# Joined attention and routing stage: the two copies of the values and the routed rows take turns on ScalarE, and the maxima of the experts move ahead of an addition on VectorE

## The chip, the cores and the metric

One core of a Trainium2 chip runs the whole kernel. The metric is the device time of one execution in microseconds (us). The engines are TensorE (PE in the profile, with PEld for its weight loads), VectorE (DVE), ScalarE (ACT), GpSimd (POOL) and the queues that issue DMAs. Each engine runs its own list of instructions in order, and semaphores hold an instruction until another engine has signalled.

## The reference

Four images of 3136 tokens with 192 features pass through a tokenizer with softmax attention, and then through blocks that add to a residual `h`. The stage of this change computes the second block and the choice of experts of the third:

```python
# linear attention with a decay, added to h
q = (elu(x @ Wq) + 1) * scale; k = elu(x @ Wk) + 1; v = x @ Wv
c = clip(cumsum(log(sigmoid(x @ Wf + bf))), -20, 20)
numerator   = q . (exp(c) * cumsum(exp(-c) * k v^T))
denominator = q . (exp(c) * cumsum(exp(-c) * k)) + 1e-6
h = h + layernorm(numerator / denominator) @ Wo
# router of the mixture of experts, on the normalised h
routing = softmax(gelu(x @ w1 + b1) @ w2 + b2)      # 8 experts
topv, topi = top_k(routing, 2)
```

The experts themselves, a second attention and a last feed-forward block follow in later stages.

## The kernel before

The joined stage is `attend_route_phase`. It cuts the 12544 tokens into 28 chunks (`NC`) of 448 tokens (`CH`), each of four tiles (`TPC`) of 112 tokens. Every engine has a loop `for g in range(NC + 3)` that is written out in full, and the order of its calls is the order of the engine. In turn g the engines work on several chunks at once: attention on chunk g, the projections of chunk g+1, the normalised rows for the router (`normalise_route`, tile `xr`) of chunk g-1, the router's matmuls of chunk g-2, and the choice of experts (`choose`, `take_rank`, `places`) of chunk g-3.

What the change and the steps of the prediction touch:

- **ScalarE.** `take_n` copies the transposed attention output (`nT`). `decay` makes `dec`, which VectorE's `q_and_k` needs. `values_out(g, i)` copies half i of the values from the accumulator `pvo` to `vt`; its signal `v_out` also frees `pvo` for TensorE's next `wo_out`. `take_ex` makes the exponentials of the router's softmax. `normalise_route` writes four tiles of `xr` and copies a part of them (L957), and signals `xr_ready`. `states` copies the running state out of `pst` into `snap`, four times in a turn, and `high_x` (L1004) takes the transposed input of the next chunk.
- **TensorE.** `values` (L790) is two halves of ten matmuls. Then `wo_out` for the first two tiles (L843), `weights` (L799), `transpose_r` (L856, waits for `xr_ready`), `wo_out` for the last two tiles (L843 again), `attend` for two tiles (L820, L822, L825), `transpose_x` (L765), `rank` (L884 to L889), `attend` for the other two, `router` and `project`. Within `attend` each tile waits for the state's copy of the tile before, and its last matmul signals `num_mm`.
- **VectorE.** `mask_weights` (L1151), `add_out(g-1, 0)` (L1159), which waits for GpSimd's `rst`, `choose` (L1206 to L1216), `add_out(g-1, 1)` (L1159), which waits for the second `wo_out`, `add_bias` (L1167, adds `brow` to `h`), the statistics, `take_rank` (L1228, waits for `rank`), `low_x`, and `sums_out` (L1095, waits for `num_mm`).
- **GpSimd.** The routed rows of chunk g-4 go to memory by eight indirect DMAs (L723) in a turn, two batches of four. One batch runs after `idx` is written; `factor` (the two instructions that make `rst`) follows it, and then the second batch.

Of the kernel before, what the change touches and what calls it, by code (L numbers as in the profile page):

```python
# [17 lines left out]
D = 192  # L18
# [5 lines left out]
TPC = CH // T  # L24
# [529 lines left out]
def attend_route_phase(nc, ins, h, bns, mean, rstd, minus, eye, held, gate, slot, shift, tile_e, tile_r, down,  # L554
# [5 lines left out]
    G3 = 3  # L560
    with ExitStack() as ctx:
# [93 lines left out]
        R = {n: sem(f"{n}_3") for n in route_names}  # L655
# [4 lines left out]
        def here(g):  # L660
            return 0 <= g < NC
# [266 lines left out]
        def _(act):  # L928
# [13 lines left out]
                    act.wait_ge(S["xn_half"], g + 1)  # L942
                    nc.scalar.copy(xn[g % 2][:, :, D:256], xn[g % 2][:, :, 128:D]).then_inc(S["xn_ready"], 1)

            def normalise_route(r):

                act.wait_ge(R["off_out"], r + 1)
                if r >= G3:
                    act.wait_ge(scattered[r % G3], 16 * 2 * TPC * (r // G3))
                x = xr[r % G3]  # L950
                for q in range(TPC):
                    t = r * TPC + q
                    ac = nc.scalar.activation(x[:, q, 0:D], h[:, t, :], ACT.Identity, bias=minus[:, t:t + 1],
                                              scale=rstd[:, t:t + 1])
                ac.then_inc(R["half_out"], 1)
                act.wait_ge(R["half_out"], r + 1)
                nc.scalar.copy(x[:, :, D:256], x[:, :, 128:D]).then_inc(R["xr_ready"], 1)  # L957

            def take_r(r):
                act.wait_ge(R["rtr_mm"], r + 1)  # L960
# [25 lines left out]
            def values_out(g, i):  # L986
                act.wait_ge(S["v_mm"], 2 * g + i + 1)
                nc.scalar.copy(vt[:, 2 * i:2 * i + 2, 0:D],
                               pvo[:, i, 0:2 * VS].rearrange("p (q v) -> p q v", q=2)[:, :, 0:D]).then_inc(
                                   S["v_out"], 1)  # L990

            def decay(g):
                act.wait_ge(S["cum_out"], g + 1)
                nc.scalar.activation(dec[:], cum[:], ACT.Exp, scale=sgn[:]).then_inc(S["dec_out"], 1)
# [30 lines left out]
            for g in range(NC + 3):  # L1025
                if here(g):
                    keys_out(g)
                if here(g + 2):
                    normalise(g + 2, (0,))
                if here(g - 2):  # L1030
                    take_r(g - 2)
                if here(g + 2):
                    normalise(g + 2, (1,))
                if here(g):
                    states(g, (0,))
                if here(g + 2):
                    normalise(g + 2, (2,))
                if here(g):
                    states(g, (1,))
                if here(g + 2):  # L1040
                    normalise(g + 2, (3,))
                if here(g + 1):
                    high_x(g + 1)
                if here(g):
                    states(g, (2, 3))
                if here(g - 2):
                    take_hidden(g - 2)
                if here(g + 1):
                    gate(g + 1)
                if here(g):  # L1050
                    take_n(g)
                if here(g + 1):
                    decay(g + 1)
                    for i in range(2):
                        values_out(g + 1, i)
                if here(g - 2):
                    take_ex(g - 2)
                if here(g - 1):
                    normalise_route(g - 1)
                if g < 2:  # L1060
                    high(g)

        @block.vector
        def _(dve):
# [84 lines left out]
            def mask_weights(g):  # L1149
                dve.wait_ge(S["at_mm"], g + 1)  # L1150
                nc.vector.tensor_tensor(at[:, :, :], pat[:, 0:CH].rearrange("p (q t) -> p q t", q=TPC),  # L1151
                                        mask[:, :].unsqueeze(1).broadcast_to([T, TPC, T]), ALU.mult).then_inc(S["at_out"], 1)
# [47 lines left out]
                nc.vector.tensor_tensor(lg[:], logit, peak[:].broadcast_to([T, TPC, E]),  # L1200
                                        ALU.subtract).then_inc(R["lg_out"], 1)

            def choose(r):

                dve.wait_ge(R["ex_out"], r + 1)
                nc.vector.tensor_reduce(total[:, :, 0], ex[:], AX.X, ALU.add)  # L1206
                for q in range(TPC):
                    mx = nc.vector.max(top[:, q, :], ex[:, q, :])
                link(mx)
                nc.vector.tensor_tensor(both[:], top[:, :, 0:1], top[:, :, 1:2], ALU.add)  # L1210
                for q in range(TPC):
                    mx = nc.vector.max_index(which[:, q, :], top[:, q, :], ex[:, q, :])
                link(mx)
                link(nc.vector.tensor_tensor(pick[:], number[:].unsqueeze(1).unsqueeze(1).broadcast_to([T, TPC, 2, E]),
                                             which[:, :, 0:2].unsqueeze(3).broadcast_to([T, TPC, 2, E]), ALU.is_equal))
                nc.vector.tensor_tensor(sel[:], pick[:, :, 0, :], pick[:, :, 1, :], ALU.add).then_inc(R["sel_out"], 1)  # L1216
# [69 lines left out]
            for g in range(NC + 3):  # L1286
                if here(g):
                    mask_weights(g)
                if here(g - 1):
                    add_out(g - 1, 0)  # L1290
                if here(g - 3):
                    choose(g - 3)
# [1330 lines left out]
```

## Time and profile before

| | |
|---|---|
| median of three runs | 2784.31 us (2782.99 to 2789.03) |
| profiled execution | 2790.76 us, of which span 2788.9 us |
| busy share: PE, DVE, ACT, POOL | 82%, 72%, 56%, 36% |
| `weights` to the last `idx` of the joined stage | about 880 to 1456 us of the span |
| TensorE's granted clock between 965.92 and 1319.41 us | 1.00 of full speed |
| VectorE, TensorE busy there, of 353.49 us | 307.11 us, 317.11 us |

The profile is of one execution. A row of its timeline gives the start of an instruction or a run of equal ones, its duration, and in brackets how long its engine sat idle before it and who ended the wait. "issue" and "remote" as the one who ended it mean that the profile found no releasing instruction close enough in time. The matmuls' ends are modelled.

### The profile page before, as it was taken

To read this page: it belongs to the slowest core of one execution; us is meant where nothing else is said; L and a number is where in the kernel's file an instruction comes from. 1 tells how busy PE (TensorE), PEld (TensorE's weight loads), DVE (VectorE), ACT (ScalarE), POOL (GpSimd) and SP (SyncE) were. 2 spreads that over 40 slices of the span, in tenths; PEclk is the share of its full clock that TensorE was granted. 3 is DMA by queue.
4 is the path that set the end of the run, shared out by engine and by line. 5 is a ranking of instruction groups with operands and counts; after the bars stand their busy time and mean duration, and the time that the engine had idled before them with its cause. 6 is when DMAs were issued, how large, how long until landed. Compare 5 with 4: busy or idle time off the path is not lost. (4 is left out here: it accounts for less than half of the span.)

```text
span 2788.9 us, 45419 instructions
## 1 busy us (share of the span) xinstructions
PE 2293.3 (82%) x14046; PEld 1665.0 (60%) x14047; DVE 2000.3 (72%) x5437; ACT 1550.6 (56%) x2693; POOL 996.8 (36%) x1024
## 2 busy tenths in 40 slices
PE   8999999999996888989865999926678885666665
PEld 4444444444444878888854999925576774444443
DVE  5777777777764888888853444447788877889986
ACT  2444444444444777777743566536665650777776
POOL 1100100100000355555561444468776730444443
PEclk9999999999997999999976999966787887677867
DMA  2000000000002011111125777731111100000000
GB/s 56 0 18 12 0 18 13 0 9 1 0 1 89 21 47 47 47 50 46 51 79 190 256 256 256 256 101 50 47 48 42 49 13 22 21 21 26 26 25 26
DMA packets 69143, 162.81 MB, mean 58 GB/s; under 512 B 12977, under 2 KB 32342, under 8 KB 68702
## 3 DMA queue, kind: packets, MB, share of 16 engines
q1 hardware_dynamic: 39426, 94.27, 10.3%
q0 software_dynamic: 21504, 44.99, 5.6%
q10 hardware_dynamic: 8064, 21.68, 2.6%
q8 instruction: 79, 1.29, 0.2%
q14 instruction: 70, 0.57, 0.1%
HBM read 63.98 MB, written 63.88 MB: 46 GB/s over the span
## 5 line engine op out<-in xcount | busy, mean ns | idle before, releaser
L211 ACT ACTIVATE prob<-pscore 128x896 f32<-128x896 f32 x336 | 308.1, 917 | 424.1 <-PE pscore L293 424.1
L418 DVE TENSOR_REDUCE pmax<-ppre 112x1 f32<-112x512 f32 x656 | 424.4, 686 | 162.7 <-PE ppre L260 162.6
L307 PE MATMUL pout<-prob,xkey 128*64 128x448 f32 x1344 | 328.3, 567 | 0.4 <-ACT prob L211 0.4
L260 PE MATMUL ppre<-xh,yh 49*112 49x512 f32 x656 | 291.5, 446 | 7.8 <-DVE pmax L418 4.1
L723 POOL DMA_INDIRECT rows_in<-xr,idx x224 | 231.4, 1033 | 154.4 <-DVE idx L1237 97.3
L1694 POOL DMA_INDIRECT yg<-rows_out,place x224 | 234.2, 1045 | 62.4 <-issue 62.1
L193 POOL CAST yh<-ynext 113x448 fp32r<-113x448 f32 x28 | 17.2, 616 | 668.1 <-DVE pmax L418 639.9
L260 PEld LDWEIGHTS ppre<-xh,yh 49*112 49x112 f32 x656 | 112.8, 172 | 239.8 <-issue 103.5
L293 PE MATMUL pscore<-yh,xh 49*128 49x448 f32 x700 | 241.3, 422 | 0.4 <-DVE yh L438 0.4
L2209 POOL TENSOR_TENSOR yg<-y,gout 112x512 f32<-112x512 f32 x112 | 141.3, 1273 | 259.1 <-DVE y L2442 259.1
L1544 POOL TENSOR_TENSOR zl<-z,zh 128x448 fp32r<-128x448 f32 x126 | 144.8, 1149 | 219.8 <-ACT zh L1510 210.3
L293 PE MATMUL pscore<-yh,xl 49*128 49x448 f32 x700 | 202.7, 364 | 0.0
L1564 DVE COPY yb<-py 112x384 f32<-112x384 f32 x126 | 70.2, 558 | 103.5 <-PE py L1472 103.4
L1458 PE MATMUL pz<-xth3b,wd 128*128 128x448 f32 x504 | 143.5, 387 | 0.0
L293 PE MATMUL pscore<-yl,xh 49*128 49x448 f32 x700 | 143.3, 364 | 0.0
L1772 PE MATMUL pqk<-xh,wh 128*128 128x448 f32 x168 | 76.9, 458 | 74.5 <-ACT junk L1915 34.8
L2254 PE MATMUL pyt<-eyeb,yq 112*128 112x112 bf16 x448 | 43.7, 285 | 111.5 <-ACT yq L2330 111.5
L1472 PE MATMUL py<-uph,zh 128*112 x504 | 130.9, 260 | 1.2 <-POOL zl L1544 1.2
L1472 PE MATMUL py<-upl,zh 128*112 x504 | 131.6, 261 | 0.0
L1472 PE MATMUL py<-uph,zl 128*112 x504 | 131.5, 261 | 0.0
L307 PEld LDWEIGHTS pout<-prob,xkey 128*64 128x64 f32 x1344 | 66.6, 135 | 106.0 <-issue 85.6
L293 PEld LDWEIGHTS pscore<-yh,xl 49*128 49x128 f32 x700 | 128.2, 187 | 0.8
(388 smaller groups left out, 6558.2 us busy)
## 6 DMA issues: line engine op xcount, KB each, us to landing
wd<-down SPq DMA_DIRECT2D x63, 512.0 KB, 3.0
xb<-rows_in SPq DMA_DIRECT2D x63, 448.0 KB, 3.6
rows_out<-yb ACTq DMA_DIRECT2D x63, 336.0 KB, 3.2
out<-ho SPq DMA_DIRECT2D x28, 336.0 KB, 2.8
rows_in<-zero SPq DMA_DIRECT2D x15, 448.0 KB
rows_in<-xr,idx POOLq DMA_INDIRECT x224
yg<-rows_out,place POOLq DMA_INDIRECT x224
xkey<-in_xkey SPq DMA_DIRECT2D x4, 800.0 KB, 6.7
```

Source lines behind the costliest of these rows:

```text
L211: nc.scalar.activation(prob[j % 3][:, :, :], pscore[j % 2][:, :, 0:CH], ACT.Exp).then_inc(exped, 1)
L260: pe.matmul(out[:, :], yh1[rows, q * T:(q + 1) * T], xh[b % 2][rows, block * 512:(block + 1) * 512], start=True, stop=True, tile_position= ...
L293: mm = pe.matmul(pscore[j % 2][:, i, 0:CH], x[b % 2][rows, keys], y[rows], start=(n == 0), stop=(n == 2), tile_position=(i * LO, 0))
L307: mm = pe.matmul(pout[i * LO:(i + 1) * LO, 0:CH], xkey[b % 2][:, 2 * j + i, :], prob[j % 3][:, i, :], start=(j == 0), stop=(i == 1 and j = ...
L418: nc.vector.reduce_max(pmax[:, q, 2 * block + half:2 * block + half + 1], bank(u, depth), AX.X).then_inc(pre_max, 1)
L723: nc.gpsimd.indirect_dma_start(rows_in, bass.IndirectOffsetOnAxis(ap=idx[r % G3][:, 2 * q + k:2 * q + k + 1], axis=0), xr[r % G3][:, q, :] ...
L1458: mm = pe.matmul(pz[m][:, 0:CH], wd[i][:, w, cols], x, start=(s_ == 0), stop=(s_ == 4))
L1472: mm = pe.matmul(py[i][:, q // 2, (q % 2) * D:(q % 2 + 1) * D], zz[i][m][:, cols], w[:, bass.ds(2 * e + m, 1), :], start=(m + n == 0), sto ...
L1544: nc.gpsimd.tensor_tensor(zl[i][m][:], z[m][:], zh[i][m][:].bitcast(F32), ALU.subtract).then_inc(S["zl_out"], 1)
L1694: nc.gpsimd.indirect_dma_start(yg[g % 2][:, q, k, :], None, rows_out, bass.IndirectOffsetOnAxis(ap=place[:, c:c + 1], axis=0)).then_inc(ga ...
L1772: mm = pe.matmul(pqk[m % 2][:, 0:CH], w, x, start=(n == 0), stop=(n == 4))
L2209: nc.gpsimd.tensor_tensor(yg[:, q, :], y[:, q, :], gout[:], ALU.mult).then_inc(S["yg_out"], 1)
```

## The change

On ScalarE the first copy of the values goes ahead of the decay. `normalise_route` is cut in two, tiles 0 and 1 and tiles 2 and 3, and the second copy of the values goes between them. The exponentials of the router (`take_ex`) so come ahead of the second copy. On VectorE the head of `choose` becomes a function of its own, `largest`: the sum of the exponentials, the eight largest of each tile and the sum of the two largest. It goes ahead of `add_out(g-1, 0)`. No instruction is added or taken away.

```diff
-            def normalise_route(r):
+            def normalise_route(r, tiles):
 
-                act.wait_ge(R["off_out"], r + 1)
-                if r >= G3:
-                    act.wait_ge(scattered[r % G3], 16 * 2 * TPC * (r // G3))
+                if 0 in tiles:
+                    act.wait_ge(R["off_out"], r + 1)
+                    if r >= G3:
+                        act.wait_ge(scattered[r % G3], 16 * 2 * TPC * (r // G3))
                 x = xr[r % G3]
-                for q in range(TPC):
+                for q in tiles:
...
-                ac.then_inc(R["half_out"], 1)
-                act.wait_ge(R["half_out"], r + 1)
-                nc.scalar.copy(x[:, :, D:256], x[:, :, 128:D]).then_inc(R["xr_ready"], 1)
+                if TPC - 1 in tiles:
+                    ac.then_inc(R["half_out"], 1)
+                    act.wait_ge(R["half_out"], r + 1)
+                    nc.scalar.copy(x[:, :, D:256], x[:, :, 128:D]).then_inc(R["xr_ready"], 1)
...
                 if here(g + 1):
+                    values_out(g + 1, 0)
                     decay(g + 1)
-                    for i in range(2):
-                        values_out(g + 1, i)
                 if here(g - 2):
                     take_ex(g - 2)
                 if here(g - 1):
-                    normalise_route(g - 1)
+                    normalise_route(g - 1, (0, 1))
+                if here(g + 1):
+                    values_out(g + 1, 1)
+                if here(g - 1):
+                    normalise_route(g - 1, (2, 3))
...
-            def choose(r):
+            def largest(r):
...
                 nc.vector.tensor_tensor(both[:], top[:, :, 0:1], top[:, :, 1:2], ALU.add)
+
+            def choose(r):
+
                 for q in range(TPC):
                     mx = nc.vector.max_index(which[:, q, :], top[:, q, :], ex[:, q, :])
...
                 if here(g):
                     mask_weights(g)
+                if here(g - 3):
+                    largest(g - 3)
                 if here(g - 1):
                     add_out(g - 1, 0)
```

On ScalarE, at the end of one turn in the middle of the stage, this stood before (`vt` are the values, `xr` the routed rows, `ktok` the keys of the next turn):

```order
L975 COPY nT<-ptr 96x896
L994 ACTIVATE dec<-cum,sgn 128x448
L988 COPY vt<-pvo 112x2x192 x2
L971 ACTIVATE ex<-lg 112x32
L953 ACTIVATE xr_1<-h,minus,rstd 112x192 x4
L957 COPY xr_1<-xr_1 112x4x64
L998 COPY ktok<-pff 112x4x64
```

and this stands there now:

```order
L977 COPY nT<-ptr 96x896
L990 COPY vt<-pvo 112x2x192
L996 ACTIVATE dec<-cum,sgn 128x448
L973 ACTIVATE ex<-lg 112x32
L954 ACTIVATE xr_1<-h,minus,rstd 112x192 x2
L990 COPY vt<-pvo 112x2x192
L954 ACTIVATE xr_1<-h,minus,rstd 112x192 x2
L959 COPY xr_1<-xr_1 112x4x64
L1000 COPY ktok<-pff 112x4x64
```

One copy of the values moved up past the decay, the other down past `ex` and two tiles of `xr`.

On VectorE, at the start of a turn, this stood before (`at` are the masked weights, `top` and `which` the largest values and their places):

```order
L1151 TENSOR_TENSOR at<-pat,mask 112x448
L1159 SCALAR_TENSOR_TENSOR h<-pvo,rst,h 112x192 x2
L1206 TENSOR_REDUCE total<-ex 112x4
L1208 MAX top<-ex 112x8 x4
L1210 TENSOR_TENSOR both<-top 112x4
L1212 MAX_INDEX which<-top,ex 112x8 x4
L1214 TENSOR_TENSOR pick<-number,which 112x64
L1216 TENSOR_TENSOR sel<-pick 112x32
L1159 SCALAR_TENSOR_TENSOR h<-pvo,rst,h 112x192 x2
L1167 TENSOR_TENSOR h<-h,brow 112x768
```

and this stands there now:

```order
L1156 TENSOR_TENSOR at<-pat,mask 112x448
L1211 TENSOR_REDUCE total<-ex 112x4
L1213 MAX top<-ex 112x8 x4
L1215 TENSOR_TENSOR both<-top 112x4
L1164 SCALAR_TENSOR_TENSOR h<-pvo,rst,h 112x192 x2
L1220 MAX_INDEX which<-top,ex 112x8 x4
L1222 TENSOR_TENSOR pick<-number,which 112x64
L1224 TENSOR_TENSOR sel<-pick 112x32
L1164 SCALAR_TENSOR_TENSOR h<-pvo,rst,h 112x192 x2
L1172 TENSOR_TENSOR h<-h,brow 112x768
```

Three groups of short instructions moved up past the first addition to `h`; the second addition and all behind it keep their order. The lists of TensorE and GpSimd are as they were.

## Rows read from the trace of the kernel before

**Rows 1.** Timeline of VectorE, one turn: start us, duration us, instruction, [idle before, releaser].

```profile
1306.88 0.62 DVE L1146 SCALAR_TENSOR_TENSOR qt<-elu,dec 64x448 f32<-64x448 f32 x1
...
1310.70 0.74 DVE L1159 SCALAR_TENSOR_TENSOR h<-pvo,rst,h 112x192 f32<-112x192 f32 x2 [0.37 <-POOL rst L705]
1311.36 0.17 DVE L1206 TENSOR_REDUCE total<-ex 112x4 f32<-112x32 f32 x1
...
1311.93 0.09 DVE L1212 MATCH_VALUE_LOAD which<-top,ex 112x8 f32 x1
...
1313.54 0.74 DVE L1159 SCALAR_TENSOR_TENSOR h<-pvo,rst,h 112x192 f32<-112x192 f32 x2 [0.48 <-issue]
1314.32 0.96 DVE L1167 TENSOR_TENSOR h<-h,brow 112x768 f32<-112x768 f32 x1
...
1317.32 0.19 DVE L1228 TENSOR_TENSOR pos<-pat,run 112x32 f32<-112x32 f32 x1 [0.45 <-PE pat L889]
...
1319.41 0.23 DVE L1095 TENSOR_SCALAR den<-pvo 112x2 f32<-112x2 f32 x2 [0.39 <-PE pvo L825]
```

**Rows 2.** Timeline of ScalarE around the same turn's start.

```profile
1306.11 0.67 ACT L994 ACTIVATE dec<-cum,sgn 128x448 f32<-128x448 f32 x1 [0.58 <-issue]
1306.69 0.46 ACT L988 COPY vt<-pvo 112x384 f32<-112x384 f32 x1
1308.31 0.48 ACT L988 COPY vt<-pvo 112x384 f32<-112x384 f32 x1 [1.16 <-remote]
1308.69 0.23 ACT L971 ACTIVATE ex<-lg 112x32 f32<-112x32 f32 x1
1308.82 1.85 ACT L953 ACTIVATE xr<-h,minus,rstd 112x192 f32<-112x192 f32 x4
1310.70 0.41 ACT L957 COPY xr<-xr 112x256 f32<-112x256 f32 x1
```

**Rows 3.** Timeline of TensorE, same stretch; the first two rows end the halves of `values`.

```profile
1305.42 0.27 PE L790 MATMUL pvo<-wxl,xh 128*112 128x192 f32 x1
...
1306.40 0.26 PE L790 MATMUL pvo<-wxl,xh 128*112 128x192 f32 x1
1307.29 1.53 PE L843 MATMUL pvo<-wo,nT 96*112 96x192 f32 x8 [0.63 <-ACT vt L988]
...
1311.16 0.97 PE L856 MATMUL ptr<-eye,xr 112*96 112x112 f32 x8 [1.12 <-ACT xr L957]
...
1313.27 0.49 PE L820 MATMUL pst<-vt,ktok 112*128 112x193 f32 x2
```

**Rows 4.** Timeline of GpSimd: last indirect DMA of one batch, first and last of the next.

```profile
1306.52 0.94 POOL L723 DMA_INDIRECT rows_in<-xr,idx  x1 [0.31 <-issue]
...
1310.87 1.00 POOL L723 DMA_INDIRECT rows_in<-xr,idx  x1 [0.20 <-issue]
...
1314.67 1.43 POOL L723 DMA_INDIRECT rows_in<-xr,idx  x1 [0.30 <-issue]
```

**Rows 5.** Timeline of ScalarE, a turn before any indirect DMA.

```profile
935.42 0.84 ACT L988 COPY vt<-pvo 112x384 f32<-112x384 f32 x2
```

**Rows 6.** Timeline of all engines in turn 4, the first with indirect DMAs.

```profile
957.63 1.00 POOL L723 DMA_INDIRECT rows_in<-xr,idx  x1 [0.20 <-issue]
...
958.75 0.49 PE L820 MATMUL pst<-vt,ktok 112*128 112x193 f32 x2
...
960.51 0.96 DVE L1167 TENSOR_TENSOR h<-h,brow 112x768 f32<-112x768 f32 x1
...
960.75 0.93 PE L765 MATMUL ptr<-eye,xn 112*128 112x112 f32 x8
961.43 0.95 POOL L723 DMA_INDIRECT rows_in<-xr,idx  x1 [0.30 <-issue]
...
963.46 0.91 ACT L1004 CAST xh<-ptr 128x896 fp32r<-128x896 f32 x1 [1.97 <-remote]
...
965.92 0.23 DVE L1095 TENSOR_SCALAR den<-pvo 112x2 f32<-112x2 f32 x2 [0.26 <-PE pvo L825]
```

## The prediction

> **What bounds the kernel now.** I read the stage from its timeline, one engine after the other, over one turn of the loop, because the change only moves instructions inside a turn. A turn is the distance between two starts of `sums_out`. It starts at 965.92 us in turn 4 [rows 6] and at 1319.41 us in turn 22 [rows 1], so 18 turns take 353.49 us and one takes 19.64 us. The reader should see that no engine fills the turn alone. VectorE is nearest to it. It waits 0.37 us for GpSimd's `rst`, 0.48 us ahead of the second addition, 0.45 us for the rank and 0.39 us for the last attention matmul [rows 1]. What ends last there is a chain through ScalarE and TensorE. The second copy of the values starts at 1308.31, `ex` and the four tiles of `xr` follow, then the copy L957 at 1310.70, and TensorE, idle for 1.12 us, starts `transpose_r` at 1311.16 [rows 2, 3]. 2.11 us after it comes `attend` at 1313.27, and 6.14 us later `sums_out` [rows 3, 1].
>
> The head of this chain is odd. The last matmul of the second half of `values` ends at 1306.66, but the copy that waits for it starts at 1308.31, after 1.16 us of idle ScalarE [rows 3, 2]. In a turn without indirect DMAs the two copies run back to back [rows 5]. So TensorE's signal reaches ScalarE 1.65 us late while GpSimd is at its fourth indirect DMA, which starts at 1306.52 [rows 4], and the copy starts 1.79 us after that. I call this a held signal. It shows again in turn 4. `transpose_x` ends at 961.68 and the cast that waits for it starts at 963.46, after 1.97 us of idle, 2.03 us behind the start of that batch's fourth DMA at 961.43 [rows 6].
>
> **The change, part by part.**
>
> Second copy behind two tiles of `xr`. ScalarE has nothing to do while the signal is held. Now `ex` and two tiles go there: 0.13 us for `ex` (1308.69 to 1308.82), and (1310.70 - 1308.82) / 4 = 0.47 us for a tile [rows 2]. That is 1.07 us, and it fits between the decay's end and 1308.31. Behind the copy stand only two tiles: 1308.31 + 0.38 + 0.94 = 1309.63 for L957, and 0.46 us later, 1310.09, `transpose_r` can start. That is 1.07 us earlier than 1311.16. TensorE is then just through with the keys (1311.16 - 1.12 = 1310.04), so the whole amount counts. `attend` moves from 1313.27 to 1312.20. Every DMA issue keeps its place, since ScalarE issues none here. If the signal of the second half were not held, the copy would not be late, and the floor would be TensorE at about 1310.0, which is the same.
>
> First copy ahead of the decay. The decay starts at 1306.11 and `q_and_k` at 1306.88, only 0.10 us behind its end [rows 1, 2]. The first half of the values is computed at 1305.69 [rows 3]. If its signal comes at once, the copy is out of the way at 1306.07 and the decay loses nothing. If it is held too, the decay waits for up to the 0.58 us between two such starts. I take 0.2 us, nearer to the lower bound, because the first half ends before the fourth DMA starts. This falls on the path: `q_and_k`, the mask, `rst` and the second batch of DMAs (1310.87 to 1311.07) all move by it. What it gives is the 0.63 us that TensorE waits for the copy [rows 3]. That lies beside VectorE's own work until the mask, so I give it nothing.
>
> Maxima ahead of the addition. They cost 1311.93 - 1311.36 = 0.57 us and fill the 0.37 us wait for `rst`. Without that wait the first addition would start at 1310.70 - 0.37 = 1310.33. With the maxima ahead of it and the 0.2 us it starts at 1311.10, 0.4 us later than before; `attend` needs it at 1312.20, and its 0.74 us end at 1311.84, so it is hidden, by 0.36 us. Before, it took 0.66 us to the next instruction (1310.70 to 1311.36), and the rest of `choose` ran from 1311.93 to the wait at 1313.54 - 0.48 = 1313.06, that is 1.13 us [rows 1]. So the second addition starts at 1311.10 + 0.66 + 1.13 = 1312.89, 0.65 us ahead of 1313.54, and no longer waits: its matmuls move by 1.07 us. The rank is ready 1.07 us earlier as well.
>
> Sum before any new wait: `sums_out` at 1319.41 - 1.07 = 1318.34, so a turn of 19.64 - 1.07 = 18.6 us. VectorE alone would allow 19.64 - 0.37 - 0.48 - 0.45 - 0.39 + 0.2 = 18.15 us, so it does not stand in the way. There are 23 turns, 5 to 27, at about 1 us: 23 us.
>
> **What is late next.** `attend` now starts 1312.20 - 1311.07 = 1.13 us behind the first DMA of the second batch. Before it started 2.40 us behind it [rows 3, 4], so half of its signals fell behind the batch. In turn 4 the distance was 958.75 - 957.63 = 1.12 us, the same as it will be, because there the second copy was not yet held [rows 6]. And that turn was no shorter: `sums_out` came 8.29 us behind the first DMA (before: 8.54), 7.17 us behind `attend` instead of 6.14. The held signal of `transpose_x` took it all.
>
> One thing differs from turn 4. `add_bias` (L1167) reads two operands from on-chip memory, and with the maxima moved it starts at 1312.89 + 0.78 = 1313.67, just as the third DMA of the batch starts. The fourth started 3.80 us behind the first [rows 4], and a step is 1.25 us (0.94 us and 0.31 us of idle), so the third is due at 1311.07 + 2.55 = 1313.62. In the turn of the rows it ran until 1315.28, 0.61 us into the fourth DMA, and that one took 1.43 us and not 0.94; in turn 4 it ended as the fourth started, and that took 0.95 us [rows 1, 4, 6]. So 0.49 us for 0.61 us of overlap. With 0.96 us of overlap, the third DMA takes some 0.75 us more and the fourth starts at 1315.6. The Trainium skill, SBUF — State Buffer, "Who interferes with whom", says that a VectorE instruction with two inputs in SBUF contends with a GpSimd instruction that reads SBUF. The trace agrees with that for 1.43 against 0.94 us. By the page alone the price would end there, on GpSimd, and the turn would be 18.6 us; it gives no wait to TensorE's signals.
>
> **Forecast.** `transpose_x` signals in the stretched third DMA and passes or waits little. In turn 4 it started 2.00 us behind `attend` and took 0.93 us [rows 6]; the rank's matmuls and the third state's follow within about a microsecond, so that state ends about 1316.1, half a microsecond into the fourth DMA. I take it to be held to 1315.6 + 1.79 = 1317.4. Its copy comes where turn 4's came behind the cast: 965.92 - 963.46 = 2.46 us less the cast's 0.91 us leaves 1.55 us to `sums_out` [rows 6]. So `sums_out` comes at 1318.95, 0.46 us ahead of 1319.41. With turn 4's 2.03 us in place of 1.79 us it is 0.22 us. I take 0.3 us, and 23 turns make 7 us. In the stage's tail the maxima fall into a wait for `rst`, which I put at 0.5 us once, about their own length. The profiled execution took 2790.76 us, 6.45 us over the median of the runs, and the sum holds as a difference against either: 2784.3 - 7.5 = 2777 us. A measurement of this kernel tells about 0.2%, 5.6 us, from no change.
>
> **Rivals.**
>
> 1. Full gain: the stretched DMA shifts the holds and no signal that matters is caught. For it: in turn 4 `attend` ran from 958.75 to `transpose_x` at 960.75 without a hold, in the second and third DMA [rows 6]. Against: the fourth DMA caught the signal in both places above. A turn of 18.3 to 18.9 us, 17 to 30 us in all, with 23 us at its middle: 2761 us.
> 2. All taken back, as in turn 4: `sums_out` 8.29 us behind 1311.07, at 1319.36, within 0.1 us of now: 2784 us, give or take 2. For it speaks turn 4. Against it, its DMAs were not stretched.
> 3. Slower. If a signal is held until the fourth DMA has been under way for 2.03 us, and `transpose_x` is caught already in the stretched third, the cast starts at 1315.6 + 2.03 = 1317.65, and 2.46 us later, at 1320.1, comes `sums_out`. That is 0.7 us later than 1319.41, 16 us in 23 turns: 2800 us. It decides as soon as `transpose_x`'s signal, due at about 1315.1, waits for the fourth DMA. For it: in turn 4 the same signal was held, 0.25 us behind the fourth DMA's start. Against: none of the rows shows a long hold that begins ahead of it.
> 4. The reordering does nothing, because the second copy waits anyway and the first two tiles of `xr` wait for something else, `off_out` or the old rows' DMAs. Against: in the turn of the rows `xr` started the moment `ex` let it [rows 2], and nothing it needs is moved. 2784 us.
>
> **How the numbers follow.** Forecast 0.38 (2772 to 2783), full gain 0.24, all taken back 0.20, slower 0.14, nothing 0.04. Six tenths of the first and all of the second are faster by over 0.2%: 0.46. Slower: the 0.14 and 0.04 from a larger delay of the decay (0.4 us in 23 turns is 9 us) on top of the third: 0.18. Within 0.2%: 0.36. The range leaves out the better half of the full gain below, and most of the slower case above: 2758 to 2792 us.
>
> **What would show it.** In the profile after: `attend` starts 1.1 us behind the first DMA of the second batch, and not 2.4 us; ScalarE's idle of 1.16 us ahead of the second copy shrinks to 0.2 or 0.3 us; VectorE's waits for `rst` and ahead of the second addition are gone; the third DMA of the second batch takes 1.7 us; a wait of over 1 us, with "remote" or "issue" as releaser, stands ahead of the third `snap` copy or of the cast. The prediction is wrong if held signals do not follow the DMAs, or if the mean distance of two `sums_out` is outside 19.1 to 19.5 us.

## The result, and the profile after

The changed kernel takes 2764.45 us (median of four runs, 2763.42 to 2765.61); the kernel before, on the same chip, 2786.26 us (four runs, 2782.99 to 2789.03). The ratio is 0.9918, with a 95% interval of 0.9904 to 0.9932: 21.8 us faster. The profiled execution took 2763.42 us, of which the span is 2761.6 us.

| distance of two `sums_out` | before | after |
|---|---|---|
| turn 0 to 4 | 75.95 us | 78.22 us |
| turn 4 to 22, each | 19.64 us (965.92 to 1319.41) | 18.42 us (967.32 to 1298.90) |
| turn 22 to 27, each | 19.47 us | 18.04 us |

So 23 turns gave 29.1 us (450.85 us before, 421.78 us after), and the first four gave back 2.3 us. The last `sums_out` starts 27.7 us earlier, and the span is 27.3 us shorter. Of that, 4.50 us are the amount by which the profiled execution of before (2790.76 us) lay over the median of 2786.26 us, and 1.03 us the amount by which that of after lay under its own.

The timeline of VectorE in one turn after the change, which answers to [rows 1]:

```profile
1280.72 0.23 DVE L1100 TENSOR_SCALAR den<-pvo 112x2 f32<-112x2 f32 x2 [0.18 <-PE pvo L825]
...
1288.27 0.62 DVE L1151 SCALAR_TENSOR_TENSOR qt<-elu,dec 64x448 f32<-64x448 f32 x1 [0.26 <-ACT dec L996]
...
1292.20 0.74 DVE L1164 SCALAR_TENSOR_TENSOR h<-pvo,rst,h 112x192 f32<-112x192 f32 x2
...
1293.95 0.74 DVE L1164 SCALAR_TENSOR_TENSOR h<-pvo,rst,h 112x192 f32<-112x192 f32 x2
1294.72 0.96 DVE L1172 TENSOR_TENSOR h<-h,brow 112x768 f32<-112x768 f32 x1
...
1297.18 0.16 DVE L1236 TENSOR_TENSOR pos<-pat,run 112x32 f32<-112x32 f32 x1
...
1298.90 0.23 DVE L1100 TENSOR_SCALAR den<-pvo 112x2 f32<-112x2 f32 x2 [0.19 <-PE pvo L825]
```

ScalarE in the same turn, which answers to [rows 2]:

```profile
1287.12 0.48 ACT L990 COPY vt<-pvo 112x384 f32<-112x384 f32 x1 [0.51 <-PE pvo L790]
1287.50 0.67 ACT L996 ACTIVATE dec<-cum,sgn 128x448 f32<-128x448 f32 x1
1288.07 0.22 ACT L973 ACTIVATE ex<-lg 112x32 f32<-112x32 f32 x1
1288.19 0.97 ACT L954 ACTIVATE xr<-h,minus,rstd 112x192 f32<-112x192 f32 x2
1289.39 0.48 ACT L990 COPY vt<-pvo 112x384 f32<-112x384 f32 x1 [0.23 <-remote]
1289.77 0.99 ACT L954 ACTIVATE xr<-h,minus,rstd 112x192 f32<-112x192 f32 x2
1290.79 0.40 ACT L959 COPY xr<-xr 112x256 f32<-112x256 f32 x1
...
1293.88 0.32 ACT L1011 COPY snap<-pst 128x193 f32<-128x193 f32 x1 [0.28 <-PE pst L820]
```

TensorE, which answers to [rows 3]:

```profile
1291.24 0.97 PE L856 MATMUL ptr<-eye,xr 112*96 112x112 f32 x8 [0.20 <-ACT xr L959]
...
1293.36 0.49 PE L820 MATMUL pst<-vt,ktok 112*128 112x193 f32 x2
```

And GpSimd, the fourth indirect DMA of one batch, and the first, third and fourth of the next, which answers to [rows 4]:

```profile
1287.60 0.94 POOL L723 DMA_INDIRECT rows_in<-xr,idx  x1 [0.30 <-issue]
...
1292.25 0.99 POOL L723 DMA_INDIRECT rows_in<-xr,idx  x1 [0.20 <-issue]
...
1294.79 1.69 POOL L723 DMA_INDIRECT rows_in<-xr,idx  x1 [0.30 <-issue]
1296.79 0.94 POOL L723 DMA_INDIRECT rows_in<-xr,idx  x1 [0.30 <-issue]
```

Read it from the `sums_out` of the turn before, which starts at 1280.72 us here and at 1299.64 us in the kernel before. The decay comes 6.78 us behind it (before 6.47), `transpose_r` 10.52 us (11.52), `attend` 12.64 us (13.63), the next `sums_out` 18.18 us (19.77). So 0.99 us were won up to `attend`, and 0.60 us between `attend` and `sums_out` (5.54 us, before 6.14). The second copy still starts 1.79 us behind the fourth DMA, as in [rows 2, 4], but only 0.23 us of that is idle now.

The 0.60 us are in the first state's copy. It starts 0.52 us behind `attend` after the change. Before it started 1.12 us behind, with 0.87 us of idle ahead of it, and TensorE waited for it in turn:

```profile
1314.39 0.32 ACT L1009 COPY snap<-pst 128x193 f32<-128x193 f32 x1 [0.87 <-PE pst L820]
```

```profile
1314.76 0.59 PE L820 MATMUL pst<-vt,ktok 112*128 112x193 f32 x2 [0.34 <-issue]
```

```profile
1313.42 0.94 POOL L723 DMA_INDIRECT rows_in<-xr,idx  x1 [0.30 <-issue]
```

These three rows are of the kernel before: ScalarE, TensorE, and GpSimd's third DMA. By the normal 0.52 us the copy was due at 1313.79, inside that DMA. The first state's copy waited like this in eight of the 18 turns before; in the other ten it was the second state's copy, with 0.62 to 0.66 us of idle where 0.24 us is normal.

The third state is the one that the forecast let wait. In the turn of the rows above, TensorE, then ScalarE:

```profile
1296.63 0.57 PE L820 MATMUL pst<-vt,ktok 112*128 112x193 f32 x2
```

```profile
1297.24 0.32 ACT L1011 COPY snap<-pst 128x193 f32<-128x193 f32 x1
```

Its matmuls end (modelled) at 1297.20 us, 0.41 us into the fourth DMA, and the copy starts at once. It is so in 14 of the 18 turns: the copy starts 0.4 to 0.6 us behind the start of the fourth DMA.

In the four others the distance was 19.03 to 19.08 us. In three of them the forecast's hold is to be seen. ScalarE and GpSimd in the turn that ends at 1096.82 us:

```profile
1093.66 0.91 ACT L1006 CAST xh<-ptr 128x896 fp32r<-128x896 f32 x1 [0.53 <-PE ptr L765]
1095.18 0.32 ACT L1011 COPY snap<-pst 128x193 f32<-128x193 f32 x1 [0.62 <-PE pst L820]
```

```profile
1091.83 1.70 POOL L723 DMA_INDIRECT rows_in<-xr,idx  x1 [0.30 <-issue]
1093.83 0.94 POOL L723 DMA_INDIRECT rows_in<-xr,idx  x1 [0.31 <-issue]
```

The third state's copy starts 1.35 us behind the fourth DMA, and the turn is 0.8 us longer than its neighbours. I find nothing in its rows ahead of the cast that tells it from them.

The fourth long turn, which ends at 1189.51 us, is different. VectorE pauses for 0.26 us without a known reason ahead of the second addition to `h`, so that `add_bias` starts inside the third DMA and not just ahead of it. That DMA is then not stretched, the fourth starts 3.80 us behind the first instead of 4.54 us, and the signal of `transpose_x` is held. VectorE, GpSimd, ScalarE:

```profile
1184.80 0.96 DVE L1172 TENSOR_TENSOR h<-h,brow 112x768 f32<-112x768 f32 x1
```

```profile
1184.53 0.94 POOL L723 DMA_INDIRECT rows_in<-xr,idx  x1 [0.30 <-issue]
1185.78 0.94 POOL L723 DMA_INDIRECT rows_in<-xr,idx  x1 [0.30 <-issue]
```

```profile
1187.02 0.91 ACT L1006 CAST xh<-ptr 128x896 fp32r<-128x896 f32 x1 [1.20 <-PE ptr L765]
```

### The profile page after: what moved, and what is told of

It is laid out like the page before. It is cut to its first block and busy times, and to the rows that moved or that the text cites. A ratio compares the mean times of both kernels' runs of the same rounds, so it can differ in the third digit from the quotient of the medians.

```text
span 2761.6 us, 45420 instructions
## 1 busy us (share of the span) xinstructions
PE 2304.1 (83%) x14046; PEld 1669.4 (60%) x14047; DVE 1995.4 (72%) x5437; ACT 1551.1 (56%) x2693; POOL 1001.9 (36%) x1024
## 3 DMA queue, kind: packets, MB, share of 16 engines
q8 instruction: 79, 1.29, 0.2%
## 5 line engine op out<-in xcount | busy, mean ns | idle before, releaser
L723 POOL DMA_INDIRECT rows_in<-xr,idx x224 | 237.8, 1062 | 132.3 <-DVE idx L1245 73.8
```

Of the source, the lines that this page charges most:

```text
L723: nc.gpsimd.indirect_dma_start(rows_in, bass.IndirectOffsetOnAxis(ap=idx[r % G3][:, 2 * q + k:2 * q + k + 1], axis=0), xr[r % G3][:, q, :] ...
```

## The experiments

Twelve measurements of nine kernels in four sessions, each session on one chip, with runs of the kernel before beside them. "Turn" is the mean of 18 turns between the two starts of `sums_out` given (turn 4 and 22).

| session | kernel | median us | before us | ratio (95%) | starts | turn |
|---|---|---|---|---|---|---|
| A, chip 10 | ScalarE's part alone | 2747.41 | 2745.80 | 1.0004 (0.9989 to 1.0018) | 967.99, 1292.68 | 18.04 |
| A | maxima alone | 2745.79 | 2745.80 | 1.0006 (0.9991 to 1.0021) | 963.81, 1286.05 | 17.90 |
| A | second copy and maxima | 2748.65 | 2745.80 | 1.0011 (0.9999 to 1.0023) | 964.32, 1286.55 | 17.90 |
| A | first copy and maxima | 2743.16 | 2745.80 | 0.9990 (0.9972 to 1.0007) | 965.39, 1282.89 | 17.64 |
| B, chip 11 | before, no indirect DMAs | 2741.96 | 2779.55 | 0.9862 (0.9831 to 0.9893) | 964.38, 1289.08 | 18.04 |
| B | changed, no indirect DMAs | 2740.65 | 2779.55 | 0.9863 (0.9832 to 0.9894) | 965.85, 1286.70 | 17.83 |
| B | changed, one-input `add_bias` | 2772.88 | 2779.55 | 0.9972 (0.9955 to 0.9989) | 966.66, 1305.82 | 18.84 |
| B | changed, `split_low` late | 2750.43 | 2779.55 | 0.9893 (0.9865 to 0.9921) | 958.33, 1282.87 | 18.03 |
| C, chip 11 | changed | 2756.72 | 2784.43 | 0.9910 (0.9887 to 0.9934) | 965.46, 1290.73 | 18.07 |
| C | first copy and maxima | 2768.81 | 2784.43 | 0.9949 (0.9935 to 0.9963) | 963.21, 1296.59 | 18.52 |
| D, chip 10 | maxima alone | 2780.32 | 2782.57 | 0.9997 (0.9980 to 1.0013) | 964.24, 1313.57 | 19.41 |
| D | second copy and maxima | 2750.09 | 2782.57 | 0.9881 (0.9859 to 0.9904) | 963.80, 1288.49 | 18.04 |

**Session A: the parts.** Four kernels between the two. ScalarE's part alone puts the maxima back:

```diff
                 if here(g - 1):
                     add_out(g - 1, 0)
                 if here(g - 3):
+                    largest(g - 3)
                     choose(g - 3)
```

> The changed kernel with the maxima back behind the first addition, so ScalarE's part alone. Theory: the whole gain (21.8 us) comes from the second copy of the values leaving the head of the chain to transpose_r, and the maxima only fill a wait of VectorE that nothing needed. Then 17 to 22 us faster than before, a turn of 18.4 to 18.7 us. Rival: the gain needs the shifted add_bias, which stretches the third indirect DMA of the second batch. With the maxima back, add_bias starts some 0.4 us later, the overlap falls partly into the fourth DMA, and signals are held again: 5 to 12 us faster, a wait of over 1 us ahead of the cast or of a snap copy in most turns.

The maxima alone have ScalarE's order of before: `decay`, both copies, `take_ex`, the four tiles.

> The kernel before with the maxima moved, so VectorE's part alone. Theory: the second addition still waits for the second wo_out, behind transpose_r, so nothing on the path moves: within 4 us of before. Rival: the rank is ready earlier and the turn ends on VectorE, where 0.37 us of waiting for rst goes away: 5 to 9 us faster.

"Second copy and maxima" puts the first copy back:

```diff
                 if here(g + 1):
-                    values_out(g + 1, 0)
                     decay(g + 1)
+                    values_out(g + 1, 0)
```

> The changed kernel with the first copy of the values back behind the decay; the second stays between the tiles of xr. Theory: the second copy carries the gain, and the first copy's place costs the decay 0.26 us a turn and gives nothing: 20 to 28 us faster than before, as fast as the changed kernel or up to 6 us faster. Rival: the first copy ahead of the decay lets TensorE start wo_out 0.6 us earlier and that is part of the gain: 10 to 16 us faster.

"First copy and maxima" puts the second copy back:

```diff
                     values_out(g + 1, 0)
                     decay(g + 1)
+                    values_out(g + 1, 1)
...
-                    normalise_route(g - 1, (0, 1))
-                if here(g + 1):
-                    values_out(g + 1, 1)
-                if here(g - 1):
-                    normalise_route(g - 1, (2, 3))
+                    normalise_route(g - 1, (0, 1, 2, 3))
```

> The changed kernel with the second copy of the values back ahead of ex and the four tiles; the first copy stays ahead of the decay, the maxima stay moved. Theory: the second copy is held by TensorE's late signal as before, so the head of the chain is as before and the decay's delay is the only other effect: between 3 us faster and 6 us slower than before. Rival: the first copy's place is part of the gain: 5 to 12 us faster.

None of the four can be told from the kernel before, and that kernel takes 2745.8 us here (median of 35), 40 us less than where the result was measured. The first and third expectation failed; the second and fourth held, but here they would have held for any cause. With ScalarE's order of before, the two copies run back to back beside the fourth DMA. ScalarE, then GpSimd, in a turn of the maxima alone:

```profile
1167.15 0.67 ACT L996 ACTIVATE dec<-cum,sgn 128x448 f32<-128x448 f32 x1 [0.58 <-DVE cum L1137]
1167.73 0.84 ACT L990 COPY vt<-pvo 112x384 f32<-112x384 f32 x2
```

```profile
1167.56 0.94 POOL L723 DMA_INDIRECT rows_in<-xr,idx  x1 [0.30 <-issue]
```

The fourth DMA takes its 0.94 us as ever, but no signal is late. Of the kernel before there is no trace from session A, only its time. I read this as two conditions, with held signals or without; without them the change has nothing to give.

**Session B: without the DMAs, and the stretched DMA.** In two kernels the loop over `indirect_dma_start` and the waits for `scattered` are gone, and the experts' stage reads rows of zeros:

```diff
-                for q in tiles:
-                    for k in range(2):
-                        nc.gpsimd.indirect_dma_start(
...
-                src = rows(rows_in, t)
+                src = rows_in[E * REGION:E * REGION + CH].rearrange("(p q) d -> p (q d)", p=T)
```

> The kernel before without the 224 indirect DMAs of the joined stage; the experts' stage reads rows of zeros instead. Theory of held signals: ScalarE's wait of 1.16 us ahead of the second copy is gone, the two copies run back to back, and a turn takes 18.3 to 18.7 us as turn 3 of before, where no such DMAs ran (18.5 us), instead of 19.64 us. Rival: the second copy is late for another reason (the matmuls really end later than modelled, or the accumulator is read late): the wait stays near 1 us and a turn stays above 19.2 us.

> The changed kernel without the 224 indirect DMAs, the same way as the kernel above. Theory of held signals: the change only dodges the hold, so without the DMAs it is worth 0.0 to 0.4 us a turn against the kernel above, and a turn takes 18.0 to 18.4 us. Rival: the new order shortens the chain in itself: about 1 us a turn less than the kernel above.

The first row below is of ScalarE's groups of instructions in the kernel before between 965 and 1320 us, the second the same group of that kernel without the DMAs, the third of the changed kernel without them. Behind the bars stand busy time, mean ns, and idle time with its releaser.

```profile
L988 ACT COPY vt<-pvo 112x384 f32<-112x384 f32 x36 | 16.9, 470 | 20.7 <-remote 20.7
```

```profile
L979 ACT COPY vt<-pvo 112x384 f32<-112x384 f32 x40 | 16.8, 470 | 0.0
```

```profile
L981 ACT COPY vt<-pvo 112x384 f32<-112x384 f32 x40 | 18.8, 469 | 3.5 <-PE pvo L783 3.4
```

The wait of 20.7 us in 18 turns is gone with the DMAs, and the change is then worth 0.21 us a turn, which the totals (2741.96 and 2740.65 us) don't tell from nothing. The turns of 18.04 and 17.83 us are shorter than I expected (18.3 to 18.7 and 18.0 to 18.4). Session A has the same: with the DMAs but without holds a turn takes 17.6 to 18.0 us, so it is the holds that cost, and not GpSimd's time.

That the matmuls only end later than modelled is ruled out by TensorE's own list, which it runs in order. In the kernel before, the next matmuls (`wo_out`, L843) start at 1307.29, over a microsecond ahead of the copy at 1308.31 that waits for the half of `values` in front of them [rows 2, 3].

The one-input kernel leaves `brow` out of the sum:

```diff
-                nc.vector.tensor_tensor(hs, hs, brow[:].unsqueeze(1).broadcast_to([T, TPC, D]),
-                                        ALU.add).then_inc(S["bias_out"], 1)
+                nc.vector.tensor_scalar(hs, hs, 1.0, None, ALU.mult).then_inc(S["bias_out"], 1)
```

> The changed kernel with add_bias's addition of brow replaced by a multiplication of h by 1, an instruction with one input in on-chip memory instead of two; brow is left out of the sum. Theory of the stretched DMA: the third DMA of the second batch takes 0.94 us and not 1.69, the fourth starts 0.75 us earlier, and the signal of transpose_x or of the third state is caught: a wait of 1 to 2 us ahead of the cast or a snap copy in most turns, a turn of 18.8 to 19.6 us, so 5 to 25 us slower than the changed kernel. Rival: the stretch has no part in it: the turn stays at 18.4 us or falls by up to 0.3 us with the shorter instruction.

In a turn of it, VectorE, then GpSimd's third and fourth DMA of the second batch, then ScalarE, then VectorE again:

```profile
1169.01 0.56 DVE L1172 TENSOR_SCALAR h<-h 112x768 f32<-112x768 f32 x1
```

```profile
1169.09 1.30 POOL L723 DMA_INDIRECT rows_in<-xr,idx  x1 [0.30 <-issue]
1170.69 0.94 POOL L723 DMA_INDIRECT rows_in<-xr,idx  x1 [0.30 <-issue]
```

```profile
1170.80 0.91 ACT L1006 CAST xh<-ptr 128x896 fp32r<-128x896 f32 x1 [0.51 <-PE ptr L765]
1172.29 0.32 ACT L1011 COPY snap<-pst 128x193 f32<-128x193 f32 x1 [0.59 <-PE pst L820]
```

```profile
1172.25 0.19 DVE L1235 TENSOR_TENSOR pos<-pat,run 112x32 f32<-112x32 f32 x1 [1.09 <-PE pat L889]
```

The third DMA was expected to take 0.94 us, with a wait of 1 to 2 us on ScalarE. The wait there is about 0.6 us, and the DMA takes 1.29 or 1.30 us in 17 of the 18 turns, so one input stretches it too, by less, because the instruction ends earlier. What decides is the order. In the traces of this case a DMA that starts while `add_bias` runs ends about 0.8 us behind the end of `add_bias` (0.82 us here, 0.80 us in the changed kernel, 0.82 us for the fourth DMA of the kernel before), and one that was already under way when `add_bias` started keeps its 0.94 us. In the one turn left VectorE pauses as above, and the DMA takes 0.95 us.

The fourth DMA so starts 4.15 us behind the first, 0.39 us earlier than in the changed kernel. The third state's matmuls, which end at 1171.40, now fall 0.71 us into it, and their signal is held in every turn, here until 1.60 us into it. The turn is 18.84 us; the changed kernel with late `split_low`, the only other one with the DMAs in session B that has a trace, takes 18.03 us. With half of the shift gone the forecast's hold is there. VectorE waits as well: the rank's matmuls ended at 1170.98, TensorE started two later pairs at 1171.24 and 1171.57, and `pos` started at 1172.25. So it is the signals that are late and not the matmuls, and not for ScalarE alone.

The late `split_low` kernel:

```diff
-                if g < 2:
-                    split_low(g)
+                if g in (NC, NC + 1):
+                    split_low(g - NC)
```

> The changed kernel with VectorE's two split_low subtractions (2.3 us each) moved from turns 0 and 1 to turns 28 and 29, where VectorE waits. Theory: in the changed kernel TensorE's idle of 2.40 us in turn 0 was followed by matmuls at the lower clock (0.85 us where 0.49 us is due), which cost turn 0 to 1 2.7 us; with the subtraction gone from there the idle shrinks below 1 us and the clock stays up: turn 0 to 1 takes 17.5 to 18.5 us instead of 21.0, turn 1 to 2 about 2 us less: 3 to 6 us faster than the changed kernel. Rival: the clock falls anyway or the tail takes it back: within 1.5 us of the changed kernel.

In this kernel VectorE's two subtractions of 2.3 us have left the first two turns. There the changed kernel had lost time to TensorE's clock. Its matmuls in turn 0, after 2.40 us of idle, take 0.85 us for two; the same ones before, after 2.06 us, 0.49 us. The granted clock was 0.84 of full speed between 889.1 and 910.1 us, with stretches at the lower level (1.2 GHz), where it had been 1.00. TensorE in the changed kernel:

```profile
901.87 1.01 PE L820 MATMUL pst<-vt,ktok 112*128 112x193 f32 x2 [2.40 <-DVE h L1164]
902.67 0.85 PE L822 MATMUL pvo<-vt,at 112*112 112x193 f32 x2
```

And in the kernel with the late `split_low`:

```profile
899.79 0.59 PE L820 MATMUL pst<-vt,ktok 112*128 112x193 f32 x2 [0.52 <-DVE h L1164]
900.22 0.49 PE L822 MATMUL pvo<-vt,at 112*112 112x193 f32 x2
```

The clock stays at 1.00, turn 0 to 4 takes 69.43 us, against 76.88 us of the changed kernel in session C, and the stage's last instruction for the map of tiles (`tile_r`) starts at 1417.2 us, against 1424.5 us. That is 7.3 us in the stage. Not all of it is the clock: with full clock and the subtraction still there, turn 0 takes 18.33 us in the kernel before, and here, without the subtraction, 16.42 us (17.5 to 18.5 expected). Over the whole kernel the two ratios (0.9893 and 0.9910) overlap, so that it beats the changed kernel is not shown; it beats the kernel before.

**Session C: the changed kernel elsewhere.** No edit in the first; the second is the kernel with first copy and maxima again.

> The changed kernel itself, on another chip than the one that gave the result. Theory: how much the change is worth is decided by whether TensorE's signals are held during the indirect DMAs, and that differs from chip to chip. Where the kernel before takes about 2780 us (a chip that holds signals) the changed one is 20 to 30 us faster; where it takes about 2746 us (a chip that does not) the changed one is within 5 us of it, as the four parts were. Rival: the ratio is the same on every chip, 0.992, and the four parts showed nothing because only all of them together gain.

> The second copy of the values back ahead of ex and the four tiles, the rest as changed (the same kernel as the earlier one with the first copy and the maxima moved). On a chip that holds signals the theory expects the wait of over 1 us ahead of the second copy to be back and a turn of 19.4 to 19.9 us, within 5 us of the kernel before; the rival, that the first copy's place is part of the gain, expects 6 to 15 us faster than before. On a chip that does not hold them both expect what the earlier run gave: within 3 us of before, a turn of 17.6 us.

The kernel before takes 2784.43 us here, and the changed one is 27.7 us faster. That fits the theory, and the rival's fixed ratio of 0.992 as well (0.9910); session D decides between them, since there the same two parts gain that gained nothing in session A. The changed kernel itself was not run in a session without holds. The second expectation missed: 15.6 us faster by the medians, half of the gain, at the upper end of its rival (6 to 15 us). ScalarE waits 17.7 us in 19 turns ahead of the copies, and the second starts 0.97 us behind the fourth DMA (1136.04), not 1.79:

```profile
1135.53 0.48 ACT L991 COPY vt<-pvo 112x384 f32<-112x384 f32 x1 [0.42 <-PE pvo L791]
1135.91 0.67 ACT L997 ACTIVATE dec<-cum,sgn 128x448 f32<-128x448 f32 x1
1137.01 0.48 ACT L991 COPY vt<-pvo 112x384 f32<-112x384 f32 x1 [0.43 <-PE pvo L791]
```

**Session D: which part carries it.** The maxima alone and the second copy with the maxima, again, to split the rest.

> The kernel before with the maxima moved, ScalarE as before. Two runs on a chip that holds signals gave 27.7 us for the whole change and 15.6 us with the second copy back in its old place, so 12 us belong to the second copy and 15.6 us to the rest. Theory: the rest is the first copy's place (TensorE's wait of 0.63 us ahead of wo_out shortens the hold of the second copy, 1.0 us behind the fourth DMA's start where it was 1.79), so the maxima alone give 0 to 4 us and the second copy waits 1.0 us or more. Rival: the rest is the maxima, because the earlier add_bias stretches the third DMA and shifts the fourth: 10 to 16 us faster than before with the long wait of the second copy still there. On a chip that does not hold signals: within 3 us of before, as in the earlier run.

> The first copy of the values back behind the decay, the rest as changed. Theory (the first copy's place carries part of the gain): 10 to 16 us faster than before, 12 to 16 us slower than the changed kernel. Rival (the maxima carry the other part): within 4 us of the changed kernel, 24 to 30 us faster than before. On a chip that does not hold signals: within 3 us of before.

Now signals are held: the chip has the same number as in session A, and the kernel before takes 2782.57 us there instead of 2745.80 us. ScalarE in a turn of the maxima alone, beside a fourth DMA that starts at 1165.15 us:

```profile
1165.32 0.46 ACT L991 COPY vt<-pvo 112x384 f32<-112x384 f32 x1
1166.76 0.48 ACT L991 COPY vt<-pvo 112x384 f32<-112x384 f32 x1 [0.97 <-PE pvo L791]
```

The maxima alone give nothing (0.9997). The second copy with the maxima gives the whole gain (0.9881, 32.5 us by the medians), so the theory's 10 to 16 us fell, and the rival's reason for its number, the maxima, fell too. The parts don't add up: with the second copy out of the way the first one's place adds nothing that can be told between the sessions (a turn of 18.04 us without it, 18.07 us with it), and only where the second stays at the head of the chain does it shorten the hold.

One turn of that kernel has its third DMA unstretched (0.94 us), and it is the one that is long, 18.64 us, with the third state held. GpSimd, then ScalarE:

```profile
1175.59 0.94 POOL L724 DMA_INDIRECT rows_in<-xr,idx  x1 [0.30 <-issue]
1176.83 0.94 POOL L724 DMA_INDIRECT rows_in<-xr,idx  x1 [0.31 <-issue]
```

```profile
1178.80 0.32 ACT L1012 COPY snap<-pst 128x193 f32<-128x193 f32 x1 [0.59 <-PE pst L821]
```

It is the turn in which VectorE pauses. The pause alone does not cost that much: in session A, without holds, the same turn of the same kernel takes 18.07 us against 17.90 us of the turn before it. So some 0.5 us of the 0.64 us are the hold. In the late `split_low` kernel VectorE does not pause, the third DMA takes 1.70 us in this turn too, and it takes 18.04 us like the others.

## Why the prediction was right on the direction and short on the size

The sign and the range held: 2764.45 us lies between 2758 and 2792. The forecast of 2777 us took 7.5 us off, and 21.8 us came. The time is the first rival's (2761 us), and so is the mechanism in 14 of 18 turns. By its own test, a mean turn outside 19.1 to 19.5 us, the prediction was wrong: 18.42 us was measured. That the time still lay inside the range is owed to the width of the range and not to the sum.

- **The wait at the head: right.** `transpose_r` and `attend` come 1.00 and 0.99 us earlier (1.07 forecast). The second copy waits 0.23 us, and it is this copy that carries the gain: in session D 0.9881 with its move and 0.9997 without.
- **First copy ahead of the decay: right in size.** The decay comes 0.31 us later (0.2 taken), and `q_and_k` waits 0.26 us for it. I gave the 0.63 us of TensorE's wait no value, and with the second copy moved that holds. With the second copy in its old place the first one's move, with the maxima, was worth 15.6 us in session C, which I had not seen.
- **Maxima: right as far as they stand alone.** The waits for `rst` and ahead of the second addition are gone, and by themselves they give nothing (0.9997). Whether the second copy's gain needs them was not run where signals are held. ScalarE's part alone ran in session A only, where its third DMA took 0.94 us. In the changed kernel it is the maxima that bring `add_bias` ahead of the third DMA, and the turns without that stretch are 0.5 to 0.8 us longer, so a part of the gain probably needs them.
- **The stretched third DMA: right.** 1.7 us forecast, 1.69 us measured; `attend` starts 1.11 us behind the first DMA (1.13 forecast), the fourth 4.54 us behind it (4.53 forecast). The Trainium skill, SBUF — State Buffer, "Who interferes with whom", has a VectorE instruction with two inputs in SBUF contend with a GpSimd instruction that reads SBUF. The trace agrees where `add_bias` is under way as the DMA starts (1.69 us against 0.94 us); where it starts inside the DMA, nothing is added (0.94 us). With one input it was 1.29 us, so the two inputs are not the whole of it. The forecast had `add_bias` start 0.05 us behind the third DMA; it starts 0.07 us ahead of it, and this order was luck, since behind it there would have been no stretch.
- **"I take it to be held to 1315.6 + 1.79": the step that failed.** The third state's matmuls ended 0.4 us into the fourth DMA, about where the forecast had put them (half a microsecond), but they were held in three of 18 turns only; in a fourth it was the signal of `transpose_x`. Each cost 0.8 us. That a signal which falls into the fourth DMA is held to its 1.79 us was too simple a rule. The stretch, which I had weighed as a partial help for `transpose_x`, moved the fourth DMA behind that signal, and so late that the third state's came early enough in it. The one-input kernel shows it: with the DMA 0.39 us earlier the state's signal falls 0.71 us into it, is held in every turn, and the turn is 0.8 us longer.
- **"6.14 us later `sums_out`": the second fault.** I carried the distance from `attend` to `sums_out` over as fixed. It contained a hold of 0.60 us, the first state's copy in the third DMA, and that went with the change. I had also written that none of the rows shows a long hold that begins ahead of the fourth DMA; the row of that copy, which is not among them, shows one of 0.6 us.
- **Not in the prediction: the start of the stage.** Turn 0 to 4 became 2.3 us longer. Turn 0 alone grew from 18.33 to 21.00 us as TensorE's granted clock fell to 0.84.
- **Rival 2 and 3** rested on turn 4 as the pattern. Its third DMA was not stretched, which I had said, and that was what decided. The tail's 0.5 us is not to be told in the runs.

The account with the two steps put right, from measured parts: 18 turns at 19.77 - 0.99 - 0.60 = 18.18 us, four of them 0.85 us longer, give a mean of 18.37 us; 18.42 us was measured. 19.64 - 18.37 = 1.27 us in 23 turns is 29 us, less 2.3 us at the start 27 us by the profiled executions (27.3 us measured). Less the 4.50 and 1.03 us by which these two lay off their medians, it is 21 to 22 us; 21.8 us was measured.

What stays open: why signals are held in one session and not in another on a chip of the same number, with the same program and DMAs of the same duration; what decides whether a signal is held (0.14 us into the fourth DMA the second copy's always was in the kernel before, and 0.4 us into it the third state's mostly was not); why VectorE pauses in one turn; and what sets the length of a hold (0.97, 1.35, 1.61, 1.79, 1.93 and 2.03 us behind the start of the fourth DMA were seen).

## What to carry to other kernels

When an engine waits for a signal whose producer has long ended, look at what GpSimd does at that moment, and put work that is ready into the wait: here the place of one copy is worth 1.4 us a turn (19.41 us with the maxima alone, 18.04 us with the second copy moved as well). Before a distance is carried over from the profile of before, look for the waits inside it. And measure such a change in more than one session: here the second copy with the maxima was worth 32 us in one session and nothing in another, and within one session nothing hinted at the other. A kernel that doesn't depend on the condition is the gain: the maxima alone take 2745.8 us or 2780.3 us, the second copy between the tiles 2748.7 us or 2750.1 us.

## What the runs showed of the hardware

- TensorE's semaphore signals reach ScalarE late during GpSimd's batches of four indirect DMAs, by up to 1.78 us (turn 4 of the kernel before), and VectorE too (1.27 us, one-input kernel), while TensorE goes on with later matmuls. In the kernel before without the DMAs there is 0.0 us of wait ahead of 40 copies. The condition is not there in each session: none in the traces of A, holds in B, C and D and where the result was measured.
- An indirect DMA that starts while a 112x768 VectorE instruction from SBUF to SBUF runs ends about 0.8 us behind that instruction: 1.69 us for an addition of two inputs (0.96 us), 1.29 us for a multiplication of one (0.56 us). A DMA that was under way first keeps its 0.94 or 0.95 us, with either.
- TensorE at full clock idled 2.06 us in turn 0 of the kernel before and went on at 0.49 us for two matmuls, and idled 2.40 us in the changed one and went on at 0.85 us. The idle time alone does not decide it: the kernel with first copy and maxima idled 2.40 us in session C and went on at 0.49 us.
